# Sparse stages' routing on VectorE: intermediate values in a PSUM bank instead of SBUF

## The chip, the cores and the metric

One core of one Trainium2 chip runs the whole program in one launch. The metric is device time in microseconds. Engines are named as in the profile: PE is TensorE, DVE is VectorE, ACT is ScalarE, POOL is GpSimd, SP is SyncE.

## The reference

Twelve residual blocks are applied to x of shape 8 x 256 x 256, float32 (2048 tokens of 256). Six of them are sparse feed-forward stages of the same form (L1 with 8 experts, L2 with 16, L3 with 8; each twice):

```
logits = norm(x) @ router                 # 2048 x E
probs  = softmax(logits)
top_p, top_i = top_k(probs, 2)            # two experts per token
shared = act(x @ s1) * (x @ s2) @ s3      # every token (L2: gelu, not gated)
routed = sum over the two: top_p * expert[top_i](x)
x = x + 0.5 * (routed + shared)
```

The other blocks (a capacity-limited sparse block, recurrent and softmax attention, a dense block) are not touched by the change.

## The kernel before, in words

Tokens lie in 16 tiles of 128 (NT = 16, P = 128). There is no planner: each engine's list of instructions is written out in program order, and semaphores order the engines against each other. On DVE most routing operations go through `step`, which lets the next one start only after the last has signalled its end.

A sparse stage has a beginning and a loop over blocks. The change touches only the beginning, which is this:

1. PE writes the logits into PSUM bank 4 (`LOGIT`). DVE subtracts each token's maximum (`moe_shift`), ACT takes the exponential (line 1402) into the SBUF tensor `ME`.
2. `moe_first` and `moe_second` (lines 1484 and 1494) find the best and the second expert of each token through `moe_best` (line 1462): maximum, comparison, product with an order, maximum, comparison. The result is the one-hot columns `MM`; `MB` is their sum in bfloat16.
3. PE multiplies `MB` with a triangle and with ones (`moe_prefix`, line 1233) into bank 5 (`COUNT`): in columns 0 to 255 how many tokens of the tile stand before this one, from column 256 the tiles' totals. `moe_places` (line 1501) makes each token's slot number per expert in `SCN`, `moe_slots` (line 1519) picks the two that apply (`PRD`, `POS`), and splits them into a block number `BLH` and a place in the block `LOH`.
4. `moe_hot` (line 1530), in four chunks of 8 token columns, makes one-hot tiles: `HOT` (block), `AHOT` (`HOT` times the token's number) and `BHOT` (place). PE multiplies `AHOT` and `BHOT` (`moe_inverse`, line 1241), adding all chunks up in bank 4: the list of tokens by slot. DVE casts it to `IDX` (line 1558).
5. POOL gathers the rows of each block with an indirect DMA by `IDX` (line 1724), and the loop over blocks runs.

Beside this, in the same queues, runs the shared feed-forward, in `early` steps (6 in L1 and L2, 12 in L3). A step is: PE up (12 matmuls, 6 in L2), ACT activation into `SGS`, DVE product with the gate (`shared_product`, line 1565, not in L2), ACT rounding into `SHH`, low part `SHL` (line 1573: on DVE in steps 0 and 1, on POOL from step 2), PE down (12 matmuls). `moe_vector` (line 1606) interleaves: after step 0 `moe_second`, after step 1 `moe_places`, in step 2 `moe_slots` and chunk 0, in step 3 chunk 1 and `moe_experts` (`EBC`, `EBF`, `EBI`: the expert of each block), in steps 4 and 5 chunks 2 and 3, then `IDX`. PE interleaves likewise (`moe_tensor`, line 1250): prefix after the third up, the inverse products between up and down.

In stages whose weights come for the first time, POOL also splits them into high and low parts meanwhile (lines 1704 and 1706). In the sparse stages that follow another sparse stage directly (`tailed`: the first L2 and the first L3), ACT takes the high parts (line 1389), POOL the low ones. In the second pass through L1, L2 and L3 the split weights are loaded instead, and POOL has only its `SHL` there.

Bank 5 has other users: warming matmuls while the tokens are turned, and results of the block loop. Both are over, or not begun, while the routing runs.

Of the kernel before, what the change touches and what calls it, by code (L numbers as in the profile page):

```python
# [162 lines left out]
def build(nc, d, out):  # L163

    with ExitStack() as ctx:
# [1002 lines left out]
        FILLS = 8  # L1168
        LOGIT, COUNT = 4, 5
        INDEX_COL = 256  # L1170
        X_BANK, UP_BANK, TURNED_BANK, DOWN_BANK = (2, 4), (0, 1), (3, 6), (5, 7)

        def slots_of(st, e_major, E):
# [217 lines left out]
        def moe_scalar(act, st):  # L1391
            m = st.m
            if not st.tailed:
                front_scalar(act, st)
            if st.tailed:
                pieces_high(act, st, 0, min(m.J, 4))
            act.wait_ge(routed, 4 * st.moe + 1)
            if m.E + 1 == 9 and st.name == 'L3':
                nc.scalar.activation(SGT[:, :].unsqueeze(2), bank[LOGIT][:, 0:256].rearrange('p (t e) -> p t e', e=16)[:, :, 8:9], ACT.Sigmoid).then_inc(sg_done, 1)
                act.wait_ge(sg_done, st.moe - 3)  # L1400
                nc.scalar.activation(SGT[:, :], SGT[:, :], ACT.Copy, scale=0.5)
            nc.scalar.activation(ME[:, :, 0:m.E], ML1[:, :, 0:m.E], ACT.Exp).then_inc(r_exp, 1)
            act.wait_ge(xn_out, 16 * GROUPS * (st.moe + 1))
            for s in range(m.early):
                shared_scalar(act, st, s)
                if st.tailed:
                    pieces_high(act, st, pieces_by(m, s), pieces_by(m, s + 1))

            def high(b):
                act.wait_ge(b_turned, st.blocks + b + 1)  # L1410
                nc.scalar.activation(GH[:, b % DEEP, :], bank[X_BANK[b % 2]][:, 0:D], ACT.Copy).then_inc(b_xhi, 1)  # L1411

            def hidden(b):
                n = st.blocks + b
                act.wait_ge(b_up, n + 1)
                if b >= DEEP:
                    act.wait_ge(b_hturned, n - DEEP + 1)
                act_of = nc.scalar.activation(HB[:, b % DEEP, 0:m.F], bank[UP_BANK[b % 2]][:, 0:m.F], m.act)  # L1418
                act_of.then_inc(b_act if m.gated else b_hid, 1)

            def hidden_high(b):
                n = st.blocks + b
                act.wait_ge(b_hturned, n + 1)
                nc.scalar.activation(HTH[0:m.hid, b % DEEP, 0:m.HC, :],
                                     bank[TURNED_BANK[b % 2]][0:m.hid, 0:m.HC * P].rearrange('p (c t) -> p c t', t=P),
                                     ACT.Copy).then_inc(b_hhi, 1)

            for b in range(m.blocks + 2 * LAGS):
                if b < m.blocks:
                    high(b)  # L1430
                if LAGS <= b < m.blocks + LAGS:
                    hidden(b - LAGS)
                if 2 * LAGS <= b:
                    hidden_high(b - 2 * LAGS)
            if not m.gated:
                nc.scalar.sem_inc(b_act, m.blocks)
            nx = st.next
            for k in range(m.front_of(GROUPS - 1) + (4 if nx else 1)):
                if k < m.late:
                    shared_scalar(act, st, m.early + k)  # L1440
                for g in range(GROUPS if nx else 0):
                    done = m.front_of(g)
                    if k == done + 2:
                        front_high(act, nx, 2 * g)
                        front_high(act, nx, 2 * g + 1)
                    if k == done + 3 and nx.kind == 'moe':
                        logits_high(act, nx, 2 * g)
                        logits_high(act, nx, 2 * g + 1)
                    if k == done + 1:
                        front_norm(act, nx, g)  # L1450
                        if nx.kind == 'moe':
                            front_store(act, nx, g)
                    if k == done:
                        front_root(act, nx, g)
                if nx and nx.kind == 'attn2':
                    if k == m.late + 1:
                        act.wait_ge(shared_added, st.added + NW)
                        nc.scalar.dma_start(FMASK[:, :], d['fmask']).then_inc(ld_c, 16)
                    ahead2_scalar(act, ahead2_slot(m, k))


        def moe_best(st, which):

            E = st.m.E
            src = ME[:, :, 0:E] if which == 0 else MT[:, :, 0:E]
            hot = MM[:, which, :, 0:E]
            most = W12[:, which, :]
            first = MS[:, 0, :]
            order = ORD[:, 0:E].unsqueeze(1).to_broadcast([P, NT, E])
            step(nc.vector.tensor_reduce(most, src, AX.X, ALU.max))  # L1470
            step(nc.vector.tensor_tensor(hot, src, most.unsqueeze(2).to_broadcast([P, NT, E]), ALU.is_ge))
            step(nc.vector.tensor_tensor(hot, hot, order, ALU.mult))
            step(nc.vector.tensor_reduce(first, hot, AX.X, ALU.max))
            step(nc.vector.tensor_tensor(hot, hot, first.unsqueeze(2).to_broadcast([P, NT, E]), ALU.is_equal))

        def moe_shift(dve, st):

# [6 lines left out]
        def moe_first(dve, st):  # L1484

            E = st.m.E
            me = ME[:, :, 0:E]
            dve.wait_ge(r_exp, st.moe + 1)
            step(nc.vector.tensor_reduce(MS[:, 1, :], me, AX.X, ALU.add))
            step(nc.vector.reciprocal(MS[:, 1, :], MS[:, 1, :]))  # L1490
            step(nc.vector.scalar_tensor_tensor(me, me, 0.5, MS[:, 1, :].unsqueeze(2).to_broadcast([P, NT, E]), ALU.mult, ALU.mult))
            moe_best(st, 0)

        def moe_second(dve, st):

            E = st.m.E
            step(nc.vector.scalar_tensor_tensor(MT[:, :, 0:E], MM[:, 0, :, 0:E], -4.0, ME[:, :, 0:E], ALU.mult, ALU.add))
            moe_best(st, 1)
            nc.vector.tensor_tensor(MB[:, 0:E, :].rearrange('p e t -> p t e'), MM[:, 0, :, 0:E], MM[:, 1, :, 0:E], ALU.add).then_inc(routed, 1)

        def moe_places(dve, st):
# [10 lines left out]
            step(nc.vector.tensor_tensor_scan(CBE[:, 0:E], ONE16[:, 0:E], NBL[:, 0:E], 0.0, ALU.mult, ALU.add))  # L1512
            step(nc.vector.tensor_tensor(EBE[:, 0:E], CBE[:, 0:E], NBL[:, 0:E], ALU.subtract))
            step(nc.vector.tensor_tensor(SCN[:, 0:E, :], SCN[:, 0:E, :], totals, ALU.subtract))
            step(nc.vector.tensor_tensor(SCN[:, 0:E, :], SCN[:, 0:E, :], before, ALU.add))
            step(nc.vector.scalar_tensor_tensor(SCN[:, 0:E, :], EBE[:, 0:E].unsqueeze(2).to_broadcast([P, E, NT]), float(P),
                                                SCN[:, 0:E, :], ALU.mult, ALU.add))

        def moe_slots(dve, st):

            E = st.m.E
            step(nc.vector.tensor_tensor(PRD[:, :, :, 0:E], MM[:, :, :, 0:E],
                                         SCN[:, 0:E, :].rearrange('p e t -> p t e').unsqueeze(1).to_broadcast([P, 2, NT, E]), ALU.mult))
            step(nc.vector.tensor_reduce(POS[:, :].rearrange('p (c t) -> p c t', c=2), PRD[:, :, :, 0:E], AX.X, ALU.add))
            step(nc.vector.tensor_copy(POSI[:, :], POS[:, :]))
            step(nc.vector.tensor_tensor(PBI[:, :], POSI[:, :], SEVEN[:, :], ALU.logical_shift_right))
            nc.vector.tensor_tensor(BLH[:, :], PBI[:, :], ONE16[:, 0:1].to_broadcast([P, 2 * NT]), ALU.mult)
            step(nc.vector.scalar_tensor_tensor(LOH[:, :], PBI[:, :], -float(P), POS[:, :], ALU.mult, ALU.add))

        def moe_hot(dve, st, c):  # L1530

            chunks = 2 * NT // CHUNK
            cols = slice(c * CHUNK, (c + 1) * CHUNK)
            tiles = slice(c * CHUNK % NT, c * CHUNK % NT + CHUNK)
            if c >= 2:
                dve.wait_ge(r_hot_read, chunks * st.moe + c - 1)
            step(nc.vector.tensor_tensor(HOT[:, :, :], BLH[:, cols].unsqueeze(2).to_broadcast([P, CHUNK, NBP]),
                                         IOH[:, 0:NBP].unsqueeze(1).to_broadcast([P, CHUNK, NBP]), ALU.is_equal))
            step(nc.vector.tensor_tensor(AHOT[:, c % 2, :, :], HOT[:, :, :],
                                         IDH[:, tiles].unsqueeze(2).to_broadcast([P, CHUNK, NBP]), ALU.mult))  # L1540
            nc.vector.tensor_tensor(BHOT[:, c % 2, :, :], LOH[:, cols].unsqueeze(2).to_broadcast([P, CHUNK, P]),
                                    IOH[:, :].unsqueeze(1).to_broadcast([P, CHUNK, P]), ALU.is_equal).then_inc(r_hot, 1)

        def moe_experts(dve, st):
# [1602 lines left out]
```

## Time and profile before

| | |
|---|---|
| Time, median of 3 runs | 3244.33 us (3240.94 to 3247.64) |
| Span of the profiled execution | 3310.2 us, mean granted PE clock 0.924 |
| Busy share PE, DVE, ACT, POOL | 87%, 67%, 45%, 47% |
| Beginnings of the six sparse stages, logits to `IDX` | 39.8, 35.2, 48.1, 34.6, 50.5, 40.5 us |

The last row of the table is from the start of line 1481 to the end of line 1558 in the order of time. The page gives the span of the one profiled execution, from its first to its last instruction; no other time of that execution is known. The profiled execution took 66 us more than the median of the timed ones. Busy shares are averages over thirteen stages with different limits. A duration in the profile holds the time in which an operation stands still for a memory port, not the time in which it waits for a semaphore.

### The profile page before, as it was taken

The page shows a single profiled execution, that of the slowest core. Times are in us where ns is not written, and L with a number is a line of the kernel's source. Part 1 is how long each engine was busy: PE and PEld are TensorE (multiplying, and loading weights), DVE is VectorE, ACT ScalarE, POOL GpSimd, SP SyncE. Part 2 cuts the span into 40 slices and gives each one's busy share as a digit, 9 for nine tenths or more (in the row PEclk, how much of TensorE's full clock was granted, in tenths as well). Part 3 has the DMA queues.
Part 4 walks back from the last instruction along what each step waited for, and adds up shares of the span by engine and source line. Part 5 has one row for each costly group of instructions (what it writes and reads, how often), then busy time and mean ns, then how long its engine had stood idle before and what let it go on. Part 6 is the DMA issues. An engine that isn't in the chain of part 4 may idle for free. (4 is left out here: it accounts for less than half of the span.)

```text
span 3310.2 us, 60075 instructions
## 1 busy us (share of the span) xinstructions
PE 2869.5 (87%) x20922; PEld 2560.7 (77%) x20922; DVE 2213.8 (67%) x5794; ACT 1489.4 (45%) x3235; POOL 1556.3 (47%) x1511
## 2 busy tenths in 40 slices
PE   8979999999999899886897967579997858977798
PEld 6869999999999787774686947557776746956697
DVE  6767777777777677765636656478886555654655
ACT  3356565666566524335323443345444334433342
POOL 2345556555555216444401346658882547350143
PEclk9989999999999898997899977879997869988899
DMA  4022122212121302361005434600003442550533
GB/s 149 1 74 68 53 71 55 71 55 71 55 71 55 114 1 79 103 223 34 20 0 191 122 96 151 205 8 2 2 2 140 118 128 81 193 185 1 204 104 98
DMA packets 147763, 285.78 MB, mean 86 GB/s; under 512 B 20673, under 2 KB 70209, under 8 KB 144385
## 3 DMA queue, kind: packets, MB, share of 16 engines
q1 hardware_dynamic: 113458, 211.38, 19.3%
q0 software_dynamic: 21216, 57.96, 6.6%
q10 hardware_dynamic: 12816, 12.78, 1.1%
q8 instruction: 174, 2.85, 0.4%
q14 instruction: 99, 0.81, 0.1%
HBM read 191.59 MB, written 90.45 MB: 85 GB/s over the span
## 5 line engine op out<-in xcount | busy, mean ns | idle before, releaser
L1724 POOL DMA_INDIRECT MXG<-dxn,IDX x250 | 237.3, 949 | 233.9 <-PE bank L1281 174.3
L1736 POOL DMA_INDIRECT YG<-dyo,POSI x192 | 187.6, 977 | 212.7 <-DMA dyo<-YS 107.7
L2688 POOL TENSOR_SCALAR SX<-SX,MN 128x256 f32<-128x256 f32 x256 | 233.7, 929 | 46.0 <-DVE MN L2619 45.9
L1573 POOL TENSOR_TENSOR SHL<-SGS,SHH 128x512 fp32r<-128x512 f32 x36 | 49.0, 1362 | 425.0 <-ACT SHH L1375 422.8
L2619 DVE CUSTOM_DVE_ANT_0 SX<-bank,FMASK 128x128 f32<-128x128 f32 (+1 forms) x512 | 156.1, 351 | 48.1 <-PE bank L2532 48.0
L1098 POOL TENSOR_TENSOR HL<-HID,HH 128x512 fp32r<-128x512 f32 x56 | 72.4, 1292 | 241.7 <-ACT HH L1063 241.5
L546 PE MATMUL bank<-MWH,GH 128*128 x500 | 171.9, 344 | 13.2 <-DVE HB L1644 6.6
L1411 ACT ACTIVATE GH<-bank 128x256 fp32r<-128x256 f32 x250 | 96.5, 387 | 179.5 <-PE bank L1281 173.6
L546 PE MATMUL bank<-MWH,SHH 128*128 128x256 f32 x352 | 111.7, 317 | 73.6 <-POOL SHL L1573 26.5
L548 PE MATMUL bank<-MWH,GL 128*128 x500 | 156.1, 312 | 0.0
L547 PE MATMUL bank<-MWL,GH 128*128 x500 | 156.0, 312 | 0.0
L1639 DVE TENSOR_TENSOR GL<-bank,GH 128x256 fp32r<-128x256 f32 x250 | 105.5, 423 | 70.9 <-ACT GH L1411 54.1
L2591 ACT ACTIVATE PT<-bank 128x384 f32<-128x384 f32 x256 | 111.7, 490 | 79.9 <-PE bank L2541 79.5
L1988 DVE TENSOR_TENSOR VL<-bank,VH 128x512 fp32r<-128x512 f32 x128 | 82.4, 686 | 96.1 <-ACT VH L1941 96.1
L546 PE MATMUL bank<-MH,XTH 128*128 128x256 f32 x512 | 145.0, 283 | 1.1 <-DVE ML L2036 1.1
L547 PE MATMUL bank<-ML,XTH 128*128 128x256 f32 x512 | 144.9, 283 | 0.0
L548 PE MATMUL bank<-MH,XTL 128*128 128x256 f32 x512 | 144.8, 283 | 0.0
L1418 ACT ACTIVATE HB<-bank 128x176 f32<-128x176 f32 (+1 forms) x250 | 75.7, 303 | 149.3 <-PE bank L548 106.6
L2079 POOL TENSOR_TENSOR HWL<-RAW,HWH 128x640 fp32r<-128x640 f32 x68 | 115.1, 1702 | 56.6 <-DVE DEC L1984 56.4
L546 PEld LDWEIGHTS bank<-MWH,SHH 128*128 128x128 f32 x352 | 73.1, 208 | 88.0 <-issue 30.6
L546 PE MATMUL bank<-MWH,HTH 88*128 (+1 forms) x406 | 136.9, 337 | 1.6 <-DVE HTL L1648 0.9
L546 PE MATMUL bank<-XTH,MWH 128*128 128x512 f32 x320 | 134.4, 420 | 3.8 <-POOL MWL L1706 3.4
(465 smaller groups left out, 11634.0 us busy)
## 6 DMA issues: line engine op xcount, KB each, us to landing
dyo<-YS SPq DMA_DIRECT2D x250, 128.0 KB
RAW<-in_wheads SPq DMA_DIRECT2D x68, 320.0 KB
BB<-dgates SPq DMA_DIRECT2D x68, 256.0 KB, 3.6
GB<-dgates SPq DMA_DIRECT2D x68, 256.0 KB, 4.2
RAW<-in_eL SPq DMA_DIRECT2D x32, 304.0 KB
dkeptL<-MWL SPq DMA_DIRECT2D x32, 304.0 KB
dkeptL<-MWH SPq DMA_DIRECT2D x32, 304.0 KB
MWH<-dkeptL SPq DMA_DIRECT2D x8, 1216.0 KB, 13.3
```

The lines of the kernel that those rows point to most:

```text
L546: nc.tensor.matmul(o, lh, rh, start=start, stop=False)
L547: nc.tensor.matmul(o, lh, rl, start=False, stop=False)
L548: return nc.tensor.matmul(o, ll, rh, start=False, stop=stop)
L1411: nc.scalar.activation(GH[:, b % DEEP, :], bank[X_BANK[b % 2]][:, 0:D], ACT.Copy).then_inc(b_xhi, 1)
L1639: nc.vector.tensor_tensor(GL[:, b % DEEP, :], bank[X_BANK[b % 2]][:, 0:D], f32(GH[:, b % DEEP, :]), ALU.subtract).then_inc(b_xlo, 1)
L1724: nc.gpsimd.indirect_dma_start(MXG[:, n % XGS, :], None, dxn, bass.IndirectOffsetOnAxis(ap=IDX[:, b:b + 1], axis=0)).then_inc(x_in[n % XGS ...
L1736: nc.gpsimd.indirect_dma_start(YG[:, i % YGS, :], None, dyo[0:m.blocks * P, :], bass.IndirectOffsetOnAxis(ap=POSI[:, c * NT + t:c * NT + t ...
L1988: return nc.vector.tensor_tensor(VL[:, s % 2, 2 * o:2 * o + 2, :], bank[4 + o][:, :].rearrange('p (t d) -> p t d', t=2), f32(VH[:, s % 2, ...
L2079: nc.gpsimd.tensor_tensor(HWL[:, parity, part], RAW[:, slot, 0:PIECE], f32(HWH[:, parity, part]), ALU.subtract).then_inc(w_ready, 1)
L2591: nc.scalar.activation(PT[:, n % RING3, :], bank[TURNED_IN[n % 2]][:, 0:TRI], ACT.Exp, scale=-1.0).then_inc(s_exp, 1)
L2619: last = nc.vector.tensor_tensor_reduce(out=SX[:, n % RING2, part], in0=o[:, part], in1=FMASK[:, part], scale=-float(HD) ** -0.5, scalar=3 ...
L2688: nc.gpsimd.tensor_scalar(part, part, MN[:, n % RING2, 1:2], None, ALU.subtract).then_inc(s_less1, 1)
```

## The change

The exponentials go to bank 5, columns 0 to 255, instead of `ME`; the scaled ones replace them there. The hot columns of `moe_best` go to columns 256 to 511, and only the last comparison writes `MM`. The slot numbers replace the totals in bank 5 instead of `SCN`. Block numbers and places go to columns 384 and 448 instead of `BLH` and `LOH`, and `HOT` to columns 0 to 383. There the values are float32 instead of float16. The number and the order of instructions stay as they were.

```diff
@@ -1168,6 +1168,7 @@
         FILLS = 8
         LOGIT, COUNT = 4, 5
         INDEX_COL = 256
+        BLOCK_COL, PLACE_COL = 384, 448
         X_BANK, UP_BANK, TURNED_BANK, DOWN_BANK = (2, 4), (0, 1), (3, 6), (5, 7)
 
         def slots_of(st, e_major, E):
@@ -1399,7 +1400,7 @@
                 nc.scalar.activation(SGT[:, :].unsqueeze(2), bank[LOGIT][:, 0:256].rearrange('p (t e) -> p t e', e=16)[:, :, 8:9], ACT.Sigmoid).then_inc(sg_done, 1)
                 act.wait_ge(sg_done, st.moe - 3)
                 nc.scalar.activation(SGT[:, :], SGT[:, :], ACT.Copy, scale=0.5)
-            nc.scalar.activation(ME[:, :, 0:m.E], ML1[:, :, 0:m.E], ACT.Exp).then_inc(r_exp, 1)
+            nc.scalar.activation(by_token(0, m.E), ML1[:, :, 0:m.E], ACT.Exp).then_inc(r_exp, 1)
             act.wait_ge(xn_out, 16 * GROUPS * (st.moe + 1))
             for s in range(m.early):
                 shared_scalar(act, st, s)
@@ -1459,11 +1460,13 @@
                     ahead2_scalar(act, ahead2_slot(m, k))
 
 
+        def by_token(lo, E):
+            return bank[COUNT][:, lo:lo + NT * 16].rearrange('p (t e) -> p t e', e=16)[:, :, 0:E]
+
         def moe_best(st, which):
 
             E = st.m.E
-            src = ME[:, :, 0:E] if which == 0 else MT[:, :, 0:E]
-            hot = MM[:, which, :, 0:E]
+            src, hot = by_token(0, E), by_token(NT * 16, E)
             most = W12[:, which, :]
             first = MS[:, 0, :]
             order = ORD[:, 0:E].unsqueeze(1).to_broadcast([P, NT, E])
@@ -1471,7 +1474,7 @@
             step(nc.vector.tensor_tensor(hot, src, most.unsqueeze(2).to_broadcast([P, NT, E]), ALU.is_ge))
             step(nc.vector.tensor_tensor(hot, hot, order, ALU.mult))
             step(nc.vector.tensor_reduce(first, hot, AX.X, ALU.max))
-            step(nc.vector.tensor_tensor(hot, hot, first.unsqueeze(2).to_broadcast([P, NT, E]), ALU.is_equal))
+            step(nc.vector.tensor_tensor(MM[:, which, :, 0:E], hot, first.unsqueeze(2).to_broadcast([P, NT, E]), ALU.is_equal))
 
         def moe_shift(dve, st):
 
@@ -1484,7 +1487,7 @@
         def moe_first(dve, st):
 
             E = st.m.E
-            me = ME[:, :, 0:E]
+            me = by_token(0, E)
             dve.wait_ge(r_exp, st.moe + 1)
             step(nc.vector.tensor_reduce(MS[:, 1, :], me, AX.X, ALU.add))
             step(nc.vector.reciprocal(MS[:, 1, :], MS[:, 1, :]))
@@ -1494,7 +1497,7 @@
         def moe_second(dve, st):
 
             E = st.m.E
-            step(nc.vector.scalar_tensor_tensor(MT[:, :, 0:E], MM[:, 0, :, 0:E], -4.0, ME[:, :, 0:E], ALU.mult, ALU.add))
+            step(nc.vector.scalar_tensor_tensor(by_token(0, E), MM[:, 0, :, 0:E], -4.0, by_token(0, E), ALU.mult, ALU.add))
             moe_best(st, 1)
             nc.vector.tensor_tensor(MB[:, 0:E, :].rearrange('p e t -> p t e'), MM[:, 0, :, 0:E], MM[:, 1, :, 0:E], ALU.add).then_inc(routed, 1)
 
@@ -1512,33 +1515,34 @@
             step(nc.vector.tensor_tensor_scan(CBE[:, 0:E], ONE16[:, 0:E], NBL[:, 0:E], 0.0, ALU.mult, ALU.add))
             step(nc.vector.tensor_tensor(EBE[:, 0:E], CBE[:, 0:E], NBL[:, 0:E], ALU.subtract))
             step(nc.vector.tensor_tensor(SCN[:, 0:E, :], SCN[:, 0:E, :], totals, ALU.subtract))
-            step(nc.vector.tensor_tensor(SCN[:, 0:E, :], SCN[:, 0:E, :], before, ALU.add))
-            step(nc.vector.scalar_tensor_tensor(SCN[:, 0:E, :], EBE[:, 0:E].unsqueeze(2).to_broadcast([P, E, NT]), float(P),
-                                                SCN[:, 0:E, :], ALU.mult, ALU.add))
+            step(nc.vector.tensor_tensor(totals, SCN[:, 0:E, :], before, ALU.add))
+            step(nc.vector.scalar_tensor_tensor(totals, EBE[:, 0:E].unsqueeze(2).to_broadcast([P, E, NT]), float(P),
+                                                totals, ALU.mult, ALU.add))
 
         def moe_slots(dve, st):
 
             E = st.m.E
             step(nc.vector.tensor_tensor(PRD[:, :, :, 0:E], MM[:, :, :, 0:E],
-                                         SCN[:, 0:E, :].rearrange('p e t -> p t e').unsqueeze(1).to_broadcast([P, 2, NT, E]), ALU.mult))
+                                         slots_of(st, 1, E).rearrange('p e t -> p t e').unsqueeze(1).to_broadcast([P, 2, NT, E]), ALU.mult))
             step(nc.vector.tensor_reduce(POS[:, :].rearrange('p (c t) -> p c t', c=2), PRD[:, :, :, 0:E], AX.X, ALU.add))
             step(nc.vector.tensor_copy(POSI[:, :], POS[:, :]))
             step(nc.vector.tensor_tensor(PBI[:, :], POSI[:, :], SEVEN[:, :], ALU.logical_shift_right))
-            nc.vector.tensor_tensor(BLH[:, :], PBI[:, :], ONE16[:, 0:1].to_broadcast([P, 2 * NT]), ALU.mult)
-            step(nc.vector.scalar_tensor_tensor(LOH[:, :], PBI[:, :], -float(P), POS[:, :], ALU.mult, ALU.add))
+            nc.vector.tensor_tensor(bank[COUNT][:, BLOCK_COL:BLOCK_COL + 2 * NT], PBI[:, :], ONE16[:, 0:1].to_broadcast([P, 2 * NT]), ALU.mult)
+            step(nc.vector.scalar_tensor_tensor(bank[COUNT][:, PLACE_COL:PLACE_COL + 2 * NT], PBI[:, :], -float(P), POS[:, :], ALU.mult, ALU.add))
 
         def moe_hot(dve, st, c):
 
             chunks = 2 * NT // CHUNK
-            cols = slice(c * CHUNK, (c + 1) * CHUNK)
             tiles = slice(c * CHUNK % NT, c * CHUNK % NT + CHUNK)
             if c >= 2:
                 dve.wait_ge(r_hot_read, chunks * st.moe + c - 1)
-            step(nc.vector.tensor_tensor(HOT[:, :, :], BLH[:, cols].unsqueeze(2).to_broadcast([P, CHUNK, NBP]),
+            hot = bank[COUNT][:, 0:CHUNK * NBP].rearrange('p (i n) -> p i n', n=NBP)
+            blocks, places = (bank[COUNT][:, at_ + c * CHUNK:at_ + (c + 1) * CHUNK] for at_ in (BLOCK_COL, PLACE_COL))
+            step(nc.vector.tensor_tensor(hot, blocks.unsqueeze(2).to_broadcast([P, CHUNK, NBP]),
                                          IOH[:, 0:NBP].unsqueeze(1).to_broadcast([P, CHUNK, NBP]), ALU.is_equal))
-            step(nc.vector.tensor_tensor(AHOT[:, c % 2, :, :], HOT[:, :, :],
+            step(nc.vector.tensor_tensor(AHOT[:, c % 2, :, :], hot,
                                          IDH[:, tiles].unsqueeze(2).to_broadcast([P, CHUNK, NBP]), ALU.mult))
-            nc.vector.tensor_tensor(BHOT[:, c % 2, :, :], LOH[:, cols].unsqueeze(2).to_broadcast([P, CHUNK, P]),
+            nc.vector.tensor_tensor(BHOT[:, c % 2, :, :], places.unsqueeze(2).to_broadcast([P, CHUNK, P]),
                                     IOH[:, :].unsqueeze(1).to_broadcast([P, CHUNK, P]), ALU.is_equal).then_inc(r_hot, 1)
 
         def moe_experts(dve, st):
```

## Rows read from the trace of the kernel before

**Rows 1.** The page's part 1: busy us, share of the span, instructions.
```profile
PE 2869.5 (87%) x20922; PEld 2560.7 (77%) x20922; DVE 2213.8 (67%) x5794; ACT 1489.4 (45%) x3235; POOL 1556.3 (47%) x1511
```

**Rows 2.** Busy time by stretch, S3's beginning: stretch, length, busy, granted clock, DMA.
```profile
1969.00:2019.00 50.00, 31.85 (x157) 26.29 (x157) 44.25 (x56) 20.04 (x34) 31.54 (x23) 0.73 0.31 91
```

**Rows 3.** Order of time, S1, POOL and DVE: start, duration, engine, line, operation.
```profile
1319.34 1.49 POOL L1706 TENSOR_TENSOR MWL<-RAW,MWH 128x608 fp32r<-128x608 f32 x1
...
1319.76 1.22 DVE L1471 TENSOR_TENSOR MM<-ME,W 128x128 f32<-128x128 f32 x1
```

**Rows 4.** Busy time by stretch of line 1541 alone: S2, S3, S4.
```profile
1768.00:1805.00 37.00, 6.78 (x4) 1.00 0.60 252
1969.00:2019.00 50.00, 7.76 (x4) 0.73 0.31 91
2542.00:2578.00 36.00, 4.90 (x4) 0.81 0.42 177
```

**Rows 5.** The same of DVE's operations that write or read `MM`: S1 to S4.
```profile
1316.00:1358.00 42.00, 9.25 (x11) 0.91 0.12 34
1768.00:1805.00 37.00, 3.92 (x11) 1.00 0.60 252
1969.00:2019.00 50.00, 9.67 (x11) 0.73 0.31 91
2542.00:2578.00 36.00, 6.12 (x11) 0.81 0.42 177
```

**Rows 6.** Groups by line: S3's `AHOT` and `HOT`, then S4's `HOT`.
```profile
L1539 DVE TENSOR_TENSOR AHOT<-HOT,IDH 128x384 f16<-128x384 f16 x4 | 4.2, 1040 | 0.1
L1537 DVE TENSOR_TENSOR HOT<-BLH,IOH 128x384 f16<-128x384 f16 x4 | 3.3, 816 | 0.0
...
L1537 DVE TENSOR_TENSOR HOT<-BLH,IOH 128x384 f16<-128x384 f16 x4 | 2.2, 550 | 0.0
```

**Rows 7.** Groups by line, whole span: a reduction from a bank and one from SBUF.
```profile
L1481 DVE TENSOR_REDUCE MS<-bank 128x16 f32<-128x128 f32 x4 | 1.2, 292 | 15.9 <-PE bank L1194 15.9
L1489 DVE TENSOR_REDUCE MS<-ME 128x16 f32<-128x128 f32 x4 | 1.1, 286 | 7.8 <-ACT ME L1402 7.8
```

**Rows 8.** Order of time, S2: chunk 1, POOL beside it, the last product.
```profile
1789.98 1.27 POOL L1573 TENSOR_TENSOR SHL<-SGS,SHH 128x512 fp32r<-128x512 f32 x1 [4.38 <-ACT SHH L1375]
...
1790.36 1.31 DVE L1537 TENSOR_TENSOR HOT<-BLH,IOH 128x384 f16<-128x384 f16 x1
...
1798.79 0.68 DVE L1565 TENSOR_TENSOR SGS<-SGS,bank 128x512 f32<-128x512 f32 x1
```

**Rows 9.** Order of time, S1: PE's prefix sum and the scan it feeds.
```profile
1331.88 0.22 PE L1239 MATMUL bank<-MB,TRB 128*128 128x128 bf16 x1
...
1333.39 0.41 DVE L1507 TENSOR_TENSOR_SCAN SCN<-RST,bank 128x128 f32<-128x128 f32 x1
```

**Rows 10.** Order of time, S4: POOL's `SHL` of step 4 and `EBC`.
```profile
2564.97 2.36 POOL L1573 TENSOR_TENSOR SHL<-SGS,SHH 128x512 fp32r<-128x512 f32 x1 [5.97 <-ACT SHH L1375]
...
2566.11 2.04 DVE L1548 TENSOR_TENSOR EBC<-IOH,CBE 1x768 f32<-1x768 f16 x1
```

**Rows 11.** Who waited for whom in S3: us in total, times, longest.
```profile
PE bank L1246 <- DVE BHOT L1541: 5.1, 2, 3.8
```

**Rows 12.** Order of time, DVE's `SGS` products: S5's 3 and 7; S6's 3, 6, 8, 9.
```profile
2759.99 0.68 DVE L1565 TENSOR_TENSOR SGS<-SGS,bank 128x512 f32<-128x512 f32 x1
...
2781.05 0.69 DVE L1565 TENSOR_TENSOR SGS<-SGS,bank 128x512 f32<-128x512 f32 x1 [1.72 <-ACT SGS L1370]
...
3114.81 0.68 DVE L1565 TENSOR_TENSOR SGS<-SGS,bank 128x512 f32<-128x512 f32 x1
...
3128.22 0.69 DVE L1565 TENSOR_TENSOR SGS<-SGS,bank 128x512 f32<-128x512 f32 x1 [0.20 <-ACT SGS L1370]
...
3137.16 0.69 DVE L1565 TENSOR_TENSOR SGS<-SGS,bank 128x512 f32<-128x512 f32 x1 [3.67 <-ACT SGS L1370]
3141.34 0.69 DVE L1565 TENSOR_TENSOR SGS<-SGS,bank 128x512 f32<-128x512 f32 x1 [3.49 <-ACT SGS L1370]
```

## The prediction

> **What bounds the kernel now.** I read the page's busy shares first: PE is busy 87% of the span, DVE 67% [rows 1], so over the whole program DVE is not the bound. An average hides stages, so next came the windows view over the six sparse stages' beginnings, from the logits to the list of gathers (S1 to S6 in order of time: L1, L1, L2, L2, L3, L3). In S3, DVE is busy 44.25 of 50 us and PE only 31.85 at a granted clock of 0.73 [rows 2]: there DVE's routing sets the end. Third, DVE beside POOL in time: in S1 the comparison `MM<-ME,W` begins at 1319.76, takes 1.22 us, and ends when POOL's `MWL` (1319.34 + 1.49 = 1320.83) has ended [rows 3]. The same line 1471 is in S2, where POOL has little to do, among eleven operations on `MM` that take 3.92 us together; in S1 they take 9.25 [rows 5]. So an operation with two inputs in SBUF stands still while such a POOL operation runs. Fourth, the stages against each other: four BHOT operations take 4.90 us in S4 (1.225 each, no wait), 6.78 in S2 and 7.76 in S3 [rows 4]: two and three waits of 0.94. S1 repeats S2; S5 and S6 repeat S3.
>
> **What the change does, and the gross sum.** No instruction is added or removed, and none is moved. The exponentials, the hot columns, the slot counts, and the block numbers and places go to bank 5, so the exponent's scaling, the comparisons and products of `moe_best`, `PRD`, `HOT`, `AHOT` and `BHOT` keep one SBUF input. The sums that stay in SBUF alone (`MB`, `PBI`, `BLH`, `EBC`, `EBF`, `EBI`) can still stand behind POOL. What can go, by stage, is the busy time above the quiet stage of the same width:
> S1: `MM` group 9.25 - 3.92 = 5.3 [rows 5], `HOT` 0.76, `BHOT` 1.9.
> S2: `HOT` 1.31 - 0.55 = 0.76 [rows 6, 8], `BHOT` 6.78 - 4.90 = 1.9 [rows 4].
> S3: `MM` group 9.67 - 6.12 = 3.55 [rows 5]; `HOT` 3.3 - 2.2 = 1.1 and `AHOT` 4.2 - 2.2 = 2.0 (its quiet price taken as `HOT`'s) [rows 6]; `BHOT` 7.76 - 4.90 = 2.9 [rows 4]. Together 9.5.
> S5 and S6: `BHOT` 2.9 each [rows 4].
> That is some 26 us. What counts is what lies on the path to the gathers.
>
> **What of it lies on the path.**
> S2: the gathers need the last inverse product, which needs PE's last down step, which waits for POOL's `SHL`, which follows the last `SGS` product at 1798.79 [rows 8]. Before that product stand the `HOT` wait (0.76) and one `BHOT` wait (0.94); the second comes behind it, beside POOL and PE, and is worth nothing. S2: 1.7.
> S1: the same tail, 1.7. Of the 5.3 us in the `MM` group, the part before PE's prefix sum is cut short by PE: the prefix ends at 1331.88 + 0.22 = 1332.10 after a full shared step, and the scan that it feeds starts at 1333.39 [rows 9]. When DVE is early, PE is late next. S1: 1.3 + 1.7 = 3.0.
> S3: PE waits for DVE throughout, so all 9.5 count, but for the end: between the last stretch's `AHOT` and `BHOT` (about 1.9 to gain) PE waits for `BHOT` only 5.1 - 3.8 = 1.3 outside its longest wait [rows 11]; after that PE's own down steps end last. S3: 9.5 - 0.6 = 8.9.
> S4: DVE has no wait there in a changed operation, but POOL does: `SHL` starts with `BHOT` at 2564.97 and takes 2.36, and `EBC` behind it takes 2.04, ending only after it [rows 10]. With `SHL` at its quiet 1.27 [rows 8] it is over at 2566.24 and not 2567.33: S4: 1.1.
> S6: `SGS` products 3 to 6 lie 3128.22 - 3114.81 = 13.4 apart, and where DVE is idle a step is 3141.34 - 3137.16 = 4.18 [rows 12], PE's own pace; three steps are 12.5. S6: 0.9.
> S5: products 3 to 7 take 2781.05 - 2759.99 = 21.1 against 4 x 4.18 = 16.7 [rows 12], so 4.4 is the most. POOL also splits weights there and still meets `EBC` and `EBF`; I take half: 2.2.
> Sum: 3.0 + 1.7 + 8.9 + 1.1 + 2.2 + 0.9 = 17.8 us.
>
> **What the new operands cost.** Reading from PSUM has rows: a reduction over 128 columns takes 292 ns from a bank and 286 from SBUF [rows 7], 6 ns. On the paths above I count some 80 operations that now touch the bank (11 in S1, 17 in S2, 18 in S3, 15 in S4, 11 in S5, 8 in S6): 0.5 us. Writing to PSUM by DVE or ACT has no row at all in this trace. Below, an operation could gain a little; by the nearest row I bound that at minus 6 ns, or 0.5 us in all. Above, a bank that serves one column's read and write by turns would need two turns for a column where source and target are both in bank 5. A column is (1225 - 292) / (1024 - 128) = 1.04 ns [rows 4, 7], so `HOT` (384 columns) would cost 0.40 more and a 128-column operation 0.13: seventeen `HOT` (6.8), seven narrow ones (0.9) and eight of 256 columns (2.1) on the paths make 9.8 us. I take the value next to the read row, 0.5 in all, since a bank read costs the same as an SBUF read to 2%, and keep 9.8 for the range. `PRD` now walks the counts in PSUM across the tiles; its stride cost there has no row either, and one such operation a stage is at most 0.27 (256 columns twice): 1.6 us for six, taken as nothing.
> The Trainium skill, "VectorE: DVE Perf Modes", section "The TRN2 errata — SBUF-src ops pay a fixed extra latency per instruction", speaks against the change: it gives 58 cycles and one per column from SBUF but 120 from PSUM, 62 cycles or 65 ns more at its 0.96 GHz. By that, as an estimate, the 80 operations cost 5.2 us and not 0.5, and the time would be near 3232. The trace has 6 ns where the page has 65, so the sum goes without it.
>
> **The forecast.** 17.8 - 0.5 = 17.3 us. The profiled span is 3310.2 us, 2.0% above the median of 3244.33; I carry the saving over unscaled (scaled it would be 17.0): 3244.3 - 17.3 = 3227.
>
> **Rivals.**
> A, dear banks: DVE's access to a bank has a price between the rows and two turns a column, 5 to 10 us on the paths. For it: no row shows a DVE write to PSUM. Against it: the reads. At two turns: 17.8 - 9.8 = 8.0, or 3236. (The page named above would land within this rival.)
> B, the waits move: DVE reaches `MB`, `PBI`, `BLH`, `EBC` and `EBF` earlier and meets POOL's operations there. A new wait costs on average half a POOL operation, 0.75 [rows 3]. Ten such waits, six of them in S3 and S5 where POOL works without pause, take 7.5: 3235. For it: POOL's queue is what it was, and these keep two SBUF inputs. Against it: they meet POOL today as well, so as many waits can go as come.
> C, slower: every operation with a bank as source or target ends later, because its semaphore comes only when the write has landed in PSUM, and the next one in `moe_best` waits for each. It decides from 17.8 / 80 = 0.22 us an operation, when a 0.29 us one takes over 0.51. At 0.32 the loss is 25.6 - 17.8 = 7.8: 3252. For it: each step waits for the one before. Against it, though only for reads: the reduction from a bank is no longer [rows 7].
> D, it doesn't do what it says: POOL's waits come from something else than the second SBUF input. Then nothing changes, 3244. Against it: bank-fed reductions average 292 ns over four stages, S1 and S5 with POOL at work among them [rows 7].
>
> **Chances.** Forecast (3219 to 3233) 0.62; A 0.14; B 0.14; C 0.07; D 0.03. A measurement of this kernel tells 0.2% (6.5 us) from no change. The forecast is faster by more; A and B are so in a little over half of their cases: faster 0.78. D and the rest of A and B: same 0.15. C: slower 0.07. The range 3214 to 3240 holds the forecast with S3 and S5 better than taken (S5 at its 4.4; PE, less idle in S3, at S1's clock of 0.91 and not 0.73, which makes 25.5 of its 31.85 us [rows 2, 5]), and A and B in most cases; C, D and the tails are left out.
>
> **What would show it.** BHOT at 1.22 to 1.23 in all 24 places, `HOT` and `AHOT` near 0.55; the `MM` line 1471 near 0.29 in S1 with POOL's `MWL` running beside it; POOL's `SHL` near 1.27 in S4; S3's window about 9 us shorter, S2's 1.7. `HOT` at 0.95 would be A; `EBC`, `PBI` and `MB` with longer waits than now, B; every short operation in `moe_best` above 0.5, C. The prediction is wrong if S3 shortens by under 5 us although its waits are gone: then PE or POOL's weight splits end that stage, not DVE.

## The result, and the profile after

The changed kernel takes **3224.59 us** (median of 4 runs, 3221.86 to 3232.76) beside 3245.98 us for the kernel before on the same chip (now 4 runs, 3240.94 to 3249.56): ratio 0.9934, 95% interval 0.992 to 0.9947, or 21.4 us. Measured again beside the later experiments it was 3223.48, ratio 0.9942 (0.9926 to 0.9958). The forecast was 3227, the range 3214 to 3240.

The spans of the two first profiles can't be set against each other: 3310.2 us before, 3219.9 after, 90 us apart where the timed runs are 21 apart. The kernel before was therefore profiled once more; that execution has a span of 3238.6. What can be compared is the length of each stage's beginning, from the first reduction of the logits to TensorE's first turn of a gathered block (the transpose with which the loop over blocks begins), read from the order of time (us):

```
                 S1    S2    S3    S4    S5    S6    sum
before, 1st     43.8  38.8  52.6  38.2  75.2  65.1  313.7
before, 2nd     43.7  38.8  56.1  38.2  73.4  65.1  315.3
after, 1st      41.4  37.0  42.8  38.3  69.0  64.2  292.7
after, 2nd      41.3  37.0  45.2  38.4  69.2  62.5  293.7
mean saving      2.4   1.8  10.4  -0.2   5.2   1.8   21.3
predicted        3.0   1.7   8.9   1.1   2.2   0.9   17.8
```

So, as far as two profiles of each tell, the beginnings hold the whole gain (21.3 of 18.8 to 21.4 timed), and the excess of the first profile of before lay elsewhere. S3 differs between executions of one kernel by up to 3.5 us; its list of gathers (`IDX`) is ready at 48.1 and 48.8 before, 37.0 and 38.7 after, and the rest of the scatter is the time from the first gather's issue to the first turn (3.8 and 6.6 us before, 5.1 and 5.8 after).

Part 1 of the page after, against [rows 1]: VectorE's (DVE's) busy time falls by 21.8 us. Against the second profile of before (2223.9) it falls by 31.9; that the 21.8 is so near to the time gained is chance.

```profile
PE 2844.8 (88%) x20922; PEld 2544.1 (79%) x20922; DVE 2192.0 (68%) x5794; ACT 1495.9 (46%) x3235; POOL 1549.6 (48%) x1511
```

Busy time of all engines in the beginnings of S3, S4 and S5 (stretch, length, busy time of PE, PEld, DVE, ACT and POOL, TensorE's granted clock, DMA), first the second profile of before, then the changed kernel; the stretches of S3 and S4 begin 0.1 us behind the table's:

```profile
1945.90:2001.90 56.00, 30.11 (x167) 24.37 (x167) 46.09 (x56) 18.41 (x31) 34.12 (x26) 0.77 0.35 104
2505.40:2543.50 38.10, 27.48 (x167) 23.19 (x167) 31.86 (x56) 8.95 (x14) 8.44 (x7) 0.83 0.40 164
2679.00:2752.40 73.40, 61.83 (x347) 51.74 (x348) 43.68 (x70) 31.33 (x50) 53.64 (x36) 0.91 0.29 83
```

```profile
1941.50:1984.20 42.70, 29.68 (x167) 23.28 (x167) 34.49 (x56) 18.35 (x31) 32.31 (x26) 0.81 0.38 107
2490.80:2529.00 38.20, 28.43 (x166) 24.33 (x166) 31.39 (x56) 8.93 (x14) 7.37 (x7) 0.78 0.40 165
2665.60:2734.60 69.00, 59.70 (x346) 50.06 (x346) 38.06 (x70) 31.48 (x50) 48.69 (x35) 0.93 0.31 86
```

In S3, DVE's time goes from 46.09 to 34.49 with the same 56 operations, while TensorE's (PE's) stays at 30: the stage was DVE's, as [rows 2] said. In S5, GpSimd (POOL) also loses 5 us, though none of its instructions was changed. One of them is a gather that no longer falls into the stretch (35 instructions, not 36); the other 4 are taken up below.

An operation's quiet time, below, is what it takes with no POOL operation beside it. DVE's groups by line after (operation, times, busy us, mean ns, idle before):

```profile
L1545 DVE TENSOR_TENSOR BHOT<-bank,IOH 128x1024 f16<-128x1024 f32 x24 | 29.4, 1224 | 0.8
L1543 DVE TENSOR_TENSOR AHOT<-bank,IDH 128x384 f16<-128x384 f32 x24 | 13.4, 557 | 0.8
L1541 DVE TENSOR_TENSOR bank<-bank,IOH 128x384 f32<-128x384 f32 x24 | 13.4, 556 | 0.2
L1528 DVE CAST POSI<-POS 128x32 int32<-128x32 f32 x6 | 6.1, 1023 | 0.2
L1529 DVE TENSOR_TENSOR PBI<-POSI,SEVEN 128x32 int32<-128x32 int32 x6 | 4.8, 794 | 0.2
...
L1474 DVE TENSOR_TENSOR bank<-bank,W 128x128 f32<-128x128 f32 x8 | 2.4, 299 | 0.3
...
L1477 DVE TENSOR_TENSOR MM<-bank,MS 128x128 f32<-128x128 f32 x8 | 2.3, 291 | 0.3
...
L1525 DVE TENSOR_TENSOR PRD<-MM,bank 128x256 f32<-128x256 f32 x4 | 1.7, 414 | 0.0
...
L1484 DVE TENSOR_REDUCE MS<-bank 128x16 f32<-128x128 f32 x4 | 1.2, 292 | 13.9 <-PE bank L1195 13.9
```

All 24 `BHOT` take 1224 ns, the quiet time of [rows 4]; `AHOT` and `HOT` take 557 and 556, the quiet 550 of [rows 6]. A comparison that reads and writes one bank (line 1474) takes 299 ns and one that reads a bank and writes SBUF (line 1477) takes 291, beside the 292 of a reduction, unchanged from [rows 7].

The order of time in S1, POOL and DVE, answers to [rows 3]:

```profile
1318.42 0.30 DVE L1474 TENSOR_TENSOR bank<-bank,W 128x128 f32<-128x128 f32 x1
1318.48 1.50 POOL L1710 TENSOR_TENSOR MWL<-RAW,MWH 128x608 fp32r<-128x608 f32 x1
1318.75 0.30 DVE L1475 TENSOR_TENSOR bank<-bank,ORD 128x128 f32<-128x128 f32 x1
...
1319.74 0.83 DVE L1502 TENSOR_TENSOR MB<-MM 128x128 bf16<-128x128 f32 x1
```

The product at 1318.75 (line 1475) begins 0.27 us into `MWL` and takes its 0.30. Before, a comparison that met a `MWL` ended only with it.

### The profile page after: what moved, and what is told of

Same layout as the page of the kernel before. It is cut to its first block and busy times, and to the rows that moved or that the text cites. A ratio compares the mean times of both kernels' runs of the same rounds, so it can differ in the third digit from the quotient of the medians.

```text
span 3219.9 us, 60075 instructions
## 1 busy us (share of the span) xinstructions
PE 2844.8 (88%) x20922; PEld 2544.1 (79%) x20922; DVE 2192.0 (68%) x5794; ACT 1495.9 (46%) x3235; POOL 1549.6 (48%) x1511
## 5 line engine op out<-in xcount | busy, mean ns | idle before, releaser
L2115 POOL TENSOR_TENSOR QL<-QG,QH 128x512 fp32r<-128x512 f32 x64 | 83.4, 1303 | 106.1 <-ACT QH L1912 106.1
```

## Experiments

The microseconds gained are worked out here from the ratios, each of which is taken against runs of the kernel before in the same series. Of longer edits the core is shown.

**Each half alone.** Two kernels made from the kernel before, with one half of the change each. The first has the exponentials and best-expert columns in the bank:

```diff
-            src = ME[:, :, 0:E] if which == 0 else MT[:, :, 0:E]
-            hot = MM[:, which, :, 0:E]
+            src, hot = by_token(0, E), by_token(NT * 16, E)
```

> The kernel before with only the first half of the change: exponentials and hot columns of the two best experts in the bank (to the count MB), slot counts, block numbers and hot blocks as before. Theory (two-SBUF operations of VectorE stand behind GpSimd's, and VectorE is on the path to the gathered blocks in S1, S3 and S5): MB ends earlier by 4.4 us in S1, 3.4 in S3, 0.7 in S5 and by nothing in S2, S4, S6, as in the changed kernel; of S1's 4.4 only 1.6 reach the first hot chunk, so start to first turn of a gathered block falls by about 1.6 + 3.4 + 0.7 = 5.7 us: 3240 us, ratio 0.998. Rival (the gain is the steps' pace, set by the hot chunks, and the exponentials are hidden behind the steps' products): 3245, ratio 1.000, with S3's first turn still at 52 us.

Measured: 3239.13, ratio 0.9985 (0.9976 to 0.9994), 4.9 us. The time fits the theory; the stages fit it only in part. `MB` ends at 11.6 and 10.8 us of S1 and S3 instead of 14.6 and 14.1, but the first turns are at 43.9, 40.6, 52.7, 38.7, 73.4 and 65.2, sum 314.4, no better than before. In S3 the list of gathers is 3 to 4 us earlier (45.0) and the first gather takes 7.0 in this execution; in S1 and S2 the granted clock was 0.85 and 0.91, against 0.93 and 1.00 before. Where its 4.9 us lie can't be read from this one execution.

The second half alone has slot counts, block numbers, places and hot blocks in the bank:

```diff
-            step(nc.vector.tensor_tensor(HOT[:, :, :], BLH[:, cols].unsqueeze(2)...
+            step(nc.vector.tensor_tensor(hot, blocks.unsqueeze(2)...
-            nc.vector.tensor_tensor(BHOT[:, c % 2, :, :], LOH[:, cols].unsqueeze(2)...
+            nc.vector.tensor_tensor(BHOT[:, c % 2, :, :], places.unsqueeze(2)...
```

> The kernel before with only the second half of the change: slot counts, block numbers, places and hot blocks in the bank; exponentials and best experts in SBUF as before. Theory: what e1 doesn't give, 21 - 5.7 = about 15 us, so 3230 us, ratio 0.995 to 0.9955; start to first turn S1 43, S2 37, S3 46, S4 38, S5 69.5, S6 64.2; BHOT 1.22 us in every stage. Rival (both halves cover one another, so that either alone gives most of the gain): S3 at 43 to 44 here and at 45 in e1, 3225. Rival (the halves are nothing without one another, since the other half's waits then end last): 3240.

Measured: 3230.05, ratio 0.9963 (0.995 to 0.9976), 12.0 us; S1 to S6 41.8, 38.8, 44.4, 35.9, 71.3, 64.2. The time is the expected one; single stages miss theirs by up to 2 us either way. The two halves add up: 4.9 + 12.0 = 16.9, and the whole is 18.8 to 21.4, within the intervals. Neither rival (one half enough, or one half nothing) holds.

**One operand put back.** The changed kernel with `BHOT`'s places in SBUF again:

```diff
-            step(nc.vector.scalar_tensor_tensor(bank[COUNT][:, PLACE_COL:PLACE_COL + 2 * NT], PBI...
+            step(nc.vector.scalar_tensor_tensor(LOH[:, :], PBI...
```

> The changed kernel with one operand put back: BHOT reads its places from the f16 tile in SBUF again (LOH), so that it has two SBUF inputs; all else stays in the bank. Theory (two SBUF inputs wait for GpSimd): BHOT goes from 1.22 us in all 24 back to 1.7 on average, 1.22 in S4 and 1.7 to 1.95 in S2 and S3, and nothing else changes its duration; 4 per stage, some half of them on the path: 3 to 6 us slower than the changed kernel, 3228 to 3231 us, ratio 0.995, S3's first turn at 44.5 to 46.5 instead of 42.7. Rival (BHOT got faster because its neighbours' traffic left SBUF, or because the bank is read faster): BHOT stays near 1.22 to 1.3, 3225 us.

Measured: 3232.51, ratio 0.9969 (0.9957 to 0.998). Set against the two ratios of the changed kernel, this one operand costs 9 to 11 us, about half of the whole change and more than the 3 to 6 expected; but the interval just touches that of the changed kernel's second series (0.9926 to 0.9958), so the size is known to within some 6 us only. `BHOT`'s group:

```profile
L1545 DVE TENSOR_TENSOR BHOT<-LOH,IOH 128x1024 f16<-128x1024 f16 x24 | 39.5, 1647 | 0.8
```

The direction is the theory's (1647 ns against 1224, nothing else put back): S3's first turn is at 48.0, and S5's `SGS` products 3 to 7 lie 21.07 us apart again, as before the change (21.06 [rows 12]; 18.46 after, below). The size may not be: 10.1 us of `BHOT` came back (39.5 against 29.4) and the kernel lost about as much, where half of it had been expected to be on a path. If that holds, either nearly all of it is, or a longer `BHOT` costs something beside its own path; the next experiments bear on that.

**The same operands with a quiet POOL.** The kernel before, everything in SBUF, with the steps' `SHL` on DVE:

```diff
-LOWS_BY_VECTOR = 2
+LOWS_BY_VECTOR = 99
```

> The kernel before, all operands in SBUF, with the early steps' low parts (SHL) on VectorE instead of GpSimd, so that GpSimd has only weight pieces to make in these stretches. The whole may be slower or faster, since VectorE does 4 to 6 operations of about 0.7 us more per stage; what counts is the durations. Theory: BHOT is at 1.22 us in every stage that has no weight pieces on GpSimd beside it, HOT near 0.6 and the small casts below 0.3, though both inputs are in SBUF. Rival (PSUM is the faster memory, or SBUF is busy with other traffic): BHOT stays at 1.7 on average and 1.9 in S3.

Measured once: 3244.17, among the runs of the kernel before beside it (3236.33 to 3250.96); DVE does POOL's `SHL` here, so no gain was to be looked for. Busy time of the four `BHOT` of S1 to S6 by stretch:

```profile
1315.20:1360.40 45.20, 4.91 (x4) 0.93 0.11 31
1763.40:1804.20 40.80, 4.90 (x4) 1.00 0.54 225
1953.60:2006.80 53.20, 6.78 (x4) 0.75 0.34 104
2506.60:2544.50 37.90, 4.90 (x4) 0.87 0.40 165
2678.00:2756.40 78.40, 7.25 (x4) 0.91 0.27 76
3033.10:3097.50 64.40, 4.90 (x4) 0.97 0.39 161
```

Without one operand in PSUM, `BHOT` is at 4.90 in all four stages where POOL has no weight pieces beside it, and stays long in S3 and S5, where it has. In the second profile of before it is 6.78 in S1 and 6.79 in S2. So PSUM isn't the faster memory: the time was POOL's. How it comes about is seen in S2 of that profile of before:

```profile
1786.32 0.56 DVE L1539 TENSOR_TENSOR AHOT<-HOT,IDH 128x384 f16<-128x384 f16 x1
...
1786.55 1.44 POOL L1573 TENSOR_TENSOR SHL<-SGS,SHH 128x512 fp32r<-128x512 f32 x1 [5.09 <-ACT SHH L1375]
...
1786.91 2.17 DVE L1541 TENSOR_TENSOR BHOT<-LOH,IOH 128x1024 f16<-128x1024 f16 x1
```

`SHL` ends at 1787.99, and `BHOT` ends at 1789.08, 1.09 us later, against 1.22 alone: it did next to nothing while `SHL` ran. `SHL` itself took 1.44, not 1.27, since `AHOT` (two inputs in SBUF) was running when it began. By the Trainium skill, "SBUF — State Buffer", section "SBUF: two separate sides", GpSimd and VectorE share a pair of ports under an exclusive lock: whichever of a GpSimd operation that reads SBUF and a VectorE operation with two SBUF inputs comes first holds it for its whole length, and the other stands still. The trace agrees in both directions, except that the held operation gets a little done meanwhile: `BHOT` 0.13 us (1.22 less 1.09), and `SHL`, 0.33 us of which lie beside `AHOT`, ends only 0.17 later.

**The other direction, measured by itself.** Is POOL held up by DVE as well, and does that cost time? Two versions of the changed kernel have four more operations in the late steps of S5 and S6, where DVE is idle; the results are not used. They differ in one operand:

```diff
+                if s >= 8:
+                    step(nc.vector.tensor_tensor(BHOT[:, 0, :, :], POS[:, 0:CHUNK].unsqueeze(2)...
```

and `bank[COUNT][:, PLACE_COL:PLACE_COL + CHUNK]` for `POS` in the second.

> The changed kernel with four more operations per stage in S5 and S6 (steps 8 to 11, where VectorE has nothing else to do behind a step's product): BHOT's shape again, with an unused result, both inputs from SBUF (the slots POS and IOH). It measures the other side of the wait: GpSimd held up by VectorE. Theory: GpSimd's operation that meets one is held for up to 1.1 us, its weight pieces in S5's late steps go from 1.50 to some 2.5 us in four cases, and since the chain of waits runs through them the late steps of S5, 4.18 us apart now, become 5.0 to 5.4 us apart: first turn of S5 3 to 5 us later (72 to 74 instead of 69), S6 0 to 4 later, whole 3228 to 3232. Rival (GpSimd isn't slowed by VectorE, or has room in S5): steps stay 4.18 us apart, 3224.

> The same four operations in S5 and S6, with the one difference that the first input is the places in the bank (f32, as POS is). Theory: GpSimd's pieces stay at 1.50 us, the late steps of S5 at 4.18 us, first turn at 69, time as the changed kernel, 3224 (the operations themselves, 1.22 us each, lie in VectorE's idle time). Rival (any more work on VectorE in the late steps delays the products): as d1, 3228 to 3232.

Measured: 3232.14 with both inputs in SBUF (ratio 0.9965, 0.9952 to 0.9977), 3227.34 with one in the bank (0.9951, 0.9936 to 0.9966); the intervals overlap, and it is the profiles that tell the two apart. Order of time in S5, DVE and then POOL, first with SBUF (the last two products):

```profile
2723.53 0.69 DVE L1569 TENSOR_TENSOR SGS<-SGS,bank 128x512 f32<-128x512 f32 x1 [1.23 <-ACT SGS L1371]
2724.14 1.84 DVE L1639 TENSOR_TENSOR BHOT<-POS,IOH 128x1024 f16<-128x1024 f32 x1
2728.67 0.69 DVE L1569 TENSOR_TENSOR SGS<-SGS,bank 128x512 f32<-128x512 f32 x1 [2.69 <-ACT SGS L1371]
...
2723.40 3.94 POOL L1713 TENSOR_TENSOR MWL<-RAW,MWH 128x608 fp32r<-128x608 f32 x2
2727.30 1.27 POOL L1577 TENSOR_TENSOR SHL<-SGS,SHH 128x512 fp32r<-128x512 f32 x1
```

and two successive products with the bank:

```profile
2722.28 0.69 DVE L1569 TENSOR_TENSOR SGS<-SGS,bank 128x512 f32<-128x512 f32 x1 [2.43 <-ACT SGS L1371]
2722.89 1.22 DVE L1639 TENSOR_TENSOR BHOT<-bank,IOH 128x1024 f16<-128x1024 f32 x1
2726.46 0.69 DVE L1569 TENSOR_TENSOR SGS<-SGS,bank 128x512 f32<-128x512 f32 x1 [2.35 <-ACT SGS L1371]
...
2724.97 2.98 POOL L1713 TENSOR_TENSOR MWL<-RAW,MWH 128x608 fp32r<-128x608 f32 x2
2727.90 1.30 POOL L1577 TENSOR_TENSOR SHL<-SGS,SHH 128x512 fp32r<-128x512 f32 x1
```

Two weight pieces take 3.94 us instead of 2.98, and the last two products come 5.14 us apart instead of 4.18; the two pairs before them are 4.40 and 4.25 apart, less than the 5.0 to 5.4 expected. Behind the last product POOL's `SHL` starts 3.73 us after it instead of 1.43. S5's first turn is at 74.2 and at 69.3; S6, whose POOL has slack (64.5 and 64.2), hardly moves. So four operations on an idle engine made a stage 4.9 us longer, through the engine that they held up (1.2 us of it is the last down step, 2.93 us at a granted clock of 0.50 against 1.69 at 1.00). The second kernel's 3 us above the changed one aren't explained by S5 and S6; its S3 was at 47.1, with 7.6 us for the first gather.

**One step further.** The operations that still met POOL ([rows 10] and the cast at line 1528 above) were given a bank operand as well: slot number, its whole number and the block number first,

```diff
-            step(nc.vector.tensor_copy(POSI[:, :], POS[:, :]))
-            step(nc.vector.tensor_tensor(PBI[:, :], POSI[:, :], SEVEN[:, :], ALU.logical_shift_right))
+            nc.vector.tensor_copy(POS[:, :], place)
+            step(nc.vector.tensor_copy(whole, place))
+            step(nc.vector.tensor_tensor(block, whole, SEVEN[:, :], ALU.logical_shift_right))
```

(`place`, `whole` and `block` are columns of bank 5; `POSI` is copied to SBUF just before `IDX`),

> The changed kernel and one step more: slot number, its whole-number form, and block number live in the bank too (the slot is copied once to SBUF for LOH, and POSI is copied to SBUF behind the hot chunks, when VectorE waits for the index product). Theory: the cast falls from 1.02 us on average to 0.3, the shift from 0.79 to 0.3, the two behind it from 0.63 to 0.3, against one copy of 0.3 more: about 1.5 us a stage less up to the first hot chunk; on the path in S1, S3, S5 and in part in S2, S6: 3 to 6 us faster than the changed kernel, 3219 to 3222 us, ratio 0.992. Rival (the wait moves: the next two-SBUF operation, the experts' EBC or EBF, takes it over, as in S4): same as the changed kernel, 3225, ratio 0.9935.

then the second hot column, the running count and the experts' row too (the core of that edit):

```diff
-            step(nc.vector.tensor_reduce(EBF[:, :], ebc, AX.X, ALU.add))
+            row = bank[COUNT][0:1, 0:NBP]
+            step(nc.vector.tensor_reduce(row, ebc, AX.X, ALU.add))
```

> e5 and the rest: the second hot column goes into the other bank (copied to SBUF behind the count MB, which reads one operand from the bank), the running block count CBE and the experts' row EBF live in the bank too, so that EBC, EBF and EBI read one operand from SBUF. Theory: EBC falls from 0.8 to 1.2 us to about 0.75, EBF and EBI to 0.3 and MB from 0.75 to 1.27 down to 0.3 to 0.45; S4, where the wait had moved to EBI, now gains: start to first turn 37 or less (38.2 in the changed kernel); 1 to 4 us faster than e5: 3217 to 3221 us, ratio 0.991 to 0.992. Rival (S4 is bound by TensorE's steps at its low clock, not by VectorE): S4 stays at 38.0 to 38.2, and the whole as e5.

Measured: 3213.20, ratio 0.9911 (0.9894 to 0.9927), and 3212.04, ratio 0.9906 (0.989 to 0.9922). The changed kernel, run beside the second of them, has 0.9942 (0.9926 to 0.9958), so both are some 10 us faster than it, with an uncertainty of some 7. For the first, 3 to 6 had been expected. The second was to be 1 to 4 us faster than the first: their beginnings sum to 287.3 and 279.8 us in one execution each, but by their times the two aren't told apart. Groups of the first:

```profile
L1561 DVE TENSOR_TENSOR EBI<-EBF,SIZES 1x48 int32<-1x48 f32 x6 | 3.2, 540 | 0.2
...
L1533 DVE TENSOR_TENSOR bank<-bank,SEVEN 128x32 int32<-128x32 int32 x6 | 1.2, 200 | 0.2
...
L1532 DVE CAST bank<-bank 128x32 int32<-128x32 f32 x6 | 1.1, 189 | 0.0
```

The cast goes from 1023 to 189 ns and the shift from 794 to 200; S5 falls from 69.1 to 65.1, nearly all of it between products 2 and 3 (4.75 us instead of 8.84), where these operations stand. `EBI`, at 356 ns in the changed kernel, now takes 540: the expected rival, on one operation. S4 stays at 38.5 there. With the experts' row in the bank `EBI` is at 195 ns, and S4 is at 36.3. `MB`, which was to fall to 0.3 to 0.45 us with one operand in the bank, still takes 716 ns (128 columns) and 1268 (256): most of its length was no wait for POOL.

## Why the prediction was right, and where its steps were off

**The mechanism** was right. `BHOT`, `HOT` and `AHOT` came out at their quiet times to 10 ns, and line 1474 in S1 at 0.30 beside `MWL`. Rival D (POOL is not the cause) is ruled out by the quiet POOL and by the pair of idle operations.

**What the operands cost** was right: 6 ns were taken for a bank read, and a 128-column operation takes 291 ns with a bank as its source and 299 with a bank as source and target, beside 286 from SBUF [rows 7]: 5 to 13 ns. Rival A needed 0.13 us more for a 128-column operation and `HOT` at 0.95; they are at 0.299 and 0.556. Rival C needed short operations above 0.51. The Trainium skill, "VectorE: DVE Perf Modes", section "The TRN2 errata — SBUF-src ops pay a fixed extra latency per instruction", would have had 65 ns more for each operation, 5.2 us as an estimate; the trace disagrees, with its 5 to 13 ns. `PRD`'s stride, taken as nothing with 0.27 as its bound, was a gain: 256 columns take 414 ns where they took 602 from SBUF with a quiet POOL.

**S1 and S2** (predicted 3.0 and 1.7, found 2.4 and 1.8) came as worked out. In S1, `MB` is 4.4 us earlier and the list of gathers only 2.3: PE is late next, as the prediction said.

**S3** (8.9, found 10.4) came out well; 1.5 us is less than two executions differ by. Who waited for whom in S3 after (us in total, times, longest) has PE's wait for `BHOT` down from the 5.1 of [rows 11] (12.8 in the second profile of before, 1.6 in the second after), and a wait for the first gather of about the same size:

```profile
PE bank L1247 <- DVE BHOT L1545: 3.8, 3, 2.8
...
PE bank L1282 <- DMA MXG<-dxn,IDX: 3.4, 1, 3.4
```

**S4** (1.1, found -0.2): this step failed. It said that with `SHL` at its quiet time `EBC` would be over 1.1 us earlier. `SHL` is quiet and `EBC` is shorter (1.42, not 2.04), but the next one meets the next `SHL`:

```profile
2514.08 1.42 DVE L1552 TENSOR_TENSOR EBC<-IOH,CBE 1x768 f32<-1x768 f16 x1
...
2516.74 1.16 DVE L1557 TENSOR_TENSOR EBI<-EBF,SIZES 1x48 int32<-1x48 f32 x1
...
2513.40 1.29 POOL L1577 TENSOR_TENSOR SHL<-SGS,SHH 128x512 fp32r<-128x512 f32 x1 [6.10 <-ACT SHH L1376]
2516.53 1.30 POOL L1577 TENSOR_TENSOR SHL<-SGS,SHH 128x512 fp32r<-128x512 f32 x1 [1.84 <-ACT SHH L1376]
```

`EBI` takes 1.16 instead of 0.20. Before, these operations waited 1.10 (`EBC`, 0.94 alone) and 0.53 (`EBF`), 1.63 together; after, 0.48 and 0.96, 1.44. That is rival B, here for a whole stage. Its sign is seen elsewhere too: `POSI` takes 1023 ns on average instead of 808, and `PBI` waits in S1 in both profiles after (1.20 us, 0.19 before), though not in the two with the idle operations. What these new waits cost wasn't measured apart from the old ones; the step that took both away gained some 10 us. The kernels with `SHL` on POOL agree with it in S4: the stage is at 38.2 to 38.7 in the eight profiles where such waits are 1.4 or more together, and at 34.7, 35.9 and 36.3 in the three where they are under 0.3. In these three the granted clock is also higher (1.00, 0.85 and 0.85 against 0.78 to 0.83), so how much is the wait's and how much the clock's, and which comes first, wasn't separated.

**S5** (2.2, found 5.2): the mis-sized term. Between products 3 and 7 the saving is 21.06 - 18.46 = 2.6 [rows 12], close to the 2.2:

```profile
2692.05 0.68 DVE L1569 TENSOR_TENSOR SGS<-SGS,bank 128x512 f32<-128x512 f32 x1
...
2710.51 0.69 DVE L1569 TENSOR_TENSOR SGS<-SGS,bank 128x512 f32<-128x512 f32 x1 [1.72 <-ACT SGS L1371]
```

The rest lies outside that stretch, the only one that was looked at. Before product 3 it is 0.4 us from the second profile of before and 2.2 from the first. In the first, products 1 and 2 lie 6.5 us apart and not 4.9; so they do in three of the four profiles with the exponentials in SBUF and in none of the eight with them in the bank. The prediction had no term for S5's `MM` operations, and here such a term shows, though it wasn't tested by itself. At the end, behind the last product, 1.4 us: the last down step takes 1.69 us instead of 2.61, and the warm-up (24 matmuls) in front of the first turn 2.79 instead of 3.49; the two overlap a little. All engines in the last 7.4 and 5.6 us before the first turn, in the second profile of before and after:

```profile
2745.00:2752.40 7.40, 5.79 (x37) 5.12 (x38) 1.66 (x4) 0.82 (x2) 6.35 (x7) 0.77 0.14 42
```

```profile
2729.00:2734.60 5.60, 4.33 (x36) 3.75 (x36) 1.66 (x4) 0.47 (x1) 4.84 (x5) 1.00 0.09 26
```

The granted clock there is 1.00 (2.4 GHz) in both profiles after, and 0.77 in both before: a part of the gain is TensorE's clock, which the sum had left at nothing. What else it left out is the other direction. POOL's own groups, in the second profile of before and then after:

```profile
L1706 POOL TENSOR_TENSOR MWL<-RAW,MWH 128x608 fp32r<-128x608 f32 (+2 forms) x59 | 93.4, 1598 | 37.2 <-ACT MWH L1389 35.7
L1573 POOL TENSOR_TENSOR SHL<-SGS,SHH 128x512 fp32r<-128x512 f32 x36 | 49.2, 1365 | 428.2 <-ACT SHH L1375 426.0 <-DVE SHL L1573 2.2
```

```profile
L1710 POOL TENSOR_TENSOR MWL<-RAW,MWH 128x608 fp32r<-128x608 f32 (+2 forms) x59 | 88.4, 1515 | 37.5 <-ACT MWH L1390 35.9
L1577 POOL TENSOR_TENSOR SHL<-SGS,SHH 128x512 fp32r<-128x512 f32 x36 | 46.3, 1286 | 414.0 <-ACT SHH L1376 414.0
```

These two groups are 7.9 us shorter in sum. That such a hold lengthens S5 is shown by the idle operations; how much of S5's 5.2 it makes up is not. The one operand put back may point the same way: its 9 to 11 us are more than DVE's side of the path alone had been costed at, but its interval allows less.

**S6** (0.9): 1.8 as a mean, 0.9 in one execution and 2.6 in the other. The stretch that was predicted, products 3 to 6, is 1.1 us shorter in both; the rest lies behind the last product.

The total was close because S1 and S4 (1.9 too much together) and S3, S5 and S6 (5.4 too little) partly cancel.

## What to carry to other kernels

Where two engines stand in each other's way, count both: an operation that waits costs its own path, and one that holds costs the other engine's, even when its own engine is idle. When a wait is taken away, list the next operations of the same kind behind it; one of them may meet the same neighbour's next operation, as `EBI` did here until it was changed as well. Read a stage's length from at least two executions before explaining a microsecond or two of it.

## What was not expected of the hardware

- A cast with a single SBUF input waits for POOL too: `POSI<-POS` takes 0.18 us in the stages where POOL is quiet and 1023 ns on average in the changed kernel; bank to bank it takes 189. The Trainium skill, "SBUF — State Buffer", section "Who interferes with whom", says that a cast can take the shared ports with one input; the trace agrees.
- `PRD`'s strided walk over the counts costs nothing in PSUM and something in SBUF: over 256 columns it takes 414 ns with the counts in a bank and 602 to 611 with them in SBUF, POOL quiet or not. A 256-column comparison from a bank takes 424 to 432.
- An operation that reads and writes the same bank costs 8 ns more than one that writes SBUF (299 against 291), not a second turn.
- In S3, the first gather's issue and the first turn lie 3.4 to 7.6 us apart, over the twelve profiled executions of kernels that issue it in the same way.
